# A gated feed-forward kernel: turned rows in two buffers, and turns, first product, second product and layer in pairs within a slot

## The chip, the cores and the metric

The kernel runs on one core of a Trainium2 chip. The metric is the device time of one execution in microseconds (us), here the median of the runs shown. The engines are named as in the profile: PE (TensorE), PEld (its weight loads), ACT (ScalarE), DVE (VectorE), POOL (GpSimd, which issues the indirect transfers) and SP (SyncE, which issues nearly all the others).

## What is computed

`x` is 16 batches of 512 rows of 512 numbers; `f` is 16 x 512 x 16 and `cond` is 16 x 512. In the reference, cut to what matters:

```
z   = (x @ f[b] / 512) @ f[b].T / 16
h   = gelu(x @ W.T + fc_bias + z + cond[b])
p   = softmax(h @ w_router + b_router)          # 16 experts
idx = top_k(p, 4)
y   = sum over e in idx of relu(h @ w1[e].T + b1[e]) @ w2[e]   # each expert is 128 wide
out = x + y + b2
```

An expert's rows are not known before the router has run, so they are collected by expert and computed in tiles.

## The kernel before

Products are made to full precision from two halves: a number is rounded to a high part by ACT (`ACT.Copy` into a float32r buffer), DVE subtracts it from the number for the low part, and PE makes three products (high by high, high by low, low by high).

The work runs in **slots** `s` = 0 to 100. The first 64 slots (`SLOTS`) each take one block of 128 rows, a quarter of a batch, through the layer: `lowrank_in` (L1044, once a batch), `layer` (L1060: 13 matmuls into one of two PSUM banks `lay`), `gelu` on ACT (L556), `turn_batch` (L1081, the block transposed on PE for the router), `take_batch` on ACT (L563), and by batch the router's softmax and choice on DVE and the counts on PE. Seven slots later POOL scatters the block's rows to the lists of their four experts in HBM (`place_rows`, L463, four indirect transfers), and the list of full tiles goes to a table there.

From slot 28 (`LAG`) on, slot `s` also works on **tile** `j = s - 28` of up to 512 rows of one expert, 72 in all (`NTILE`). The first 49 (`FULL`) have one expert; the other 23 are two halves of 256 rows with an expert each. The work of a tile is spread over three slots:
- `load_tile` (L310, SP) reads its number from the table, then loads its rows (1,056 KB) into one of two buffers `gr`, and its table row into `tabi`. It is issued in SP's slot `s` for tile `j + 2`.
- `turn_tile` (PE, L1146) transposes 128 rows of tile `j + 1` into one of two banks `trn`; `take_tile` (ACT L574, DVE L741) splits them into `gsb`, which is one buffer, so that ACT waits for `p_f1`, the first product of the tile before. `split_w1` (L580, L876) splits the expert's first weights, also after `p_f1`.
- `ffn1(j)` (L1162) is the first product: 12 matmuls (24 for two experts) into the bank `hid`. `hidden` (ACT, L601) adds bias and clips; `split_hidden` and DVE's `hidden` split it into `hh` and `hl`, one buffer each.
- `ffn2(j - 1, c)` (L1188) is the second product for a quarter `c`, into one of two banks `yps`; `result` copies it to `ys` (ACT for even `c`, DVE for odd), and POOL's `send` (L490) scatters it to `yt` in HBM.

What sets the order is one loop over `s` for each engine, written out by hand, with semaphores between. PE's order in a slot:

```
lowrank_in, layer(s), positions, router, turn_batch(s-1), counts, ffn1(j),
turn_tile(j+1,0), ffn2(j-1,0), turn_tile(j+1,1), ffn2(j-1,1), turn_tile(j+1,2), ffn2(j-1,2), turn_tile(j+1,3), ffn2(j-1,3)
```

`split_x(s + 4)` splits the block of `x` that is needed next but three; it stands near the start of ACT's and DVE's slot. `x` comes through two small buffers `stx`, and SP's loop begins each slot with `load_x(s + 6)` (L276):

```
def load_x(s):
    if s >= 4:
        sp.wait_ge(v_xl, s - 3 if s < 6 else s - 1)
    sp.dma_start(stx[:, x_buffer(s), :], xT[s]).then_inc(s_x[x_buffer(s)], 16)
```

So `load_x(s + 6)` waits until `split_x(s + 4)` is done on DVE (`v_xl`). Behind it, in order, SP has `load_u` and `load_v` (every fourth slot), some small copies, and `load_tile(j + 2)`.

After the last tile comes the **tail**: 32 sums of 256 rows, each of 2,048 KB of `yt`, plus `x` (512 KB) and `b2`, and out. `x` and `b2` are prepared ahead in the buffers `xin` (24 of the 32), 12 of them (`EARLY`) loaded from slot 80 on.

## Time and profile before

| | |
|---|---|
| Median of 3 runs | 1313.26 us (1309.89 to 1313.92) |
| Profiled execution: span, first to last instruction | 1288.1 us |
| Its own time as a run | not listed; the median is 25.2 us above the span |
| Busy: PE / DVE / ACT / POOL | 911.6 / 828.0 / 584.8 / 584.3 us |
| Granted TensorE clock, mean of the span | 0.869 |
| Moved by DMA | 354.82 MB, 275 GB/s over the span |

The span falls into four stretches: slots 0 to 27, the layer and the router alone (to about 197 us); slots 28 to 63, layer and tiles together (to about 699 us); slots from 64 on, tiles alone (to about 1067 us); and the tail. In a view by stretches, each engine has its busy time and number of instructions, and behind them stand the granted clock as a share of full speed, the busy share of the DMA engines, and GB/s. In a timeline, a row is start, duration, engine, line and operation, what is written from what is read, the count, and in brackets the engine's idle time before it with what ended that. "remote" there is a releaser that the profile doesn't show.

### The profile page before, as it was taken

To read this page: it belongs to the slowest core of one execution; us is meant where nothing else is said; L and a number is where in the kernel's file an instruction comes from. 1 tells how busy PE (TensorE), PEld (TensorE's weight loads), DVE (VectorE), ACT (ScalarE), POOL (GpSimd) and SP (SyncE) were. 2 spreads that over 40 slices of the span, in tenths; PEclk is the share of its full clock that TensorE was granted. 3 is DMA by queue.
4 is the path that set the end of the run, shared out by engine and by line. 5 is a ranking of instruction groups with operands and counts; after the bars stand their busy time and mean duration, and the time that the engine had idled before them with its cause. 6 is when DMAs were issued, how large, how long until landed. Compare 5 with 4: busy or idle time off the path is not lost.

```text
span 1288.1 us, 17916 instructions
## 1 busy us (share of the span) xinstructions
PE 911.6 (71%) x4924; PEld 702.2 (55%) x4924; DVE 828.0 (64%) x1964; ACT 584.8 (45%) x1061; POOL 584.3 (45%) x589
## 2 busy tenths in 40 slices
PE   8887789889899998888898774898898981000000
PEld 7664567677677766666676553677676761000000
DVE  4444355666556665556656563877687867987777
ACT  5434345565556555465546453765566560000000
POOL 1455664555565655555565655454455543000000
PEclk9988789989999999999999896999999996555555
DMA  5777577776787777777876765787888759999999
GB/s 173 266 241 272 190 245 278 263 258 228 252 272 264 252 263 256 246 259 242 269 261 235 254 237 220 239 261 236 288 271 259 232 166 357 414 429 429 426 430 385
DMA packets 103234, 354.82 MB, mean 275 GB/s; under 512 B 29961, under 2 KB 29961, under 8 KB 92384
## 3 DMA queue, kind: packets, MB, share of 16 engines
q1 hardware_dynamic: 59104, 217.21, 49.6%
q0 software_dynamic: 43936, 136.37, 27.0%
q8 instruction: 41, 0.67, 0.2%
q14 instruction: 57, 0.47, 0.1%
q10 hardware_dynamic: 96, 0.10, 0.0%
HBM read 200.47 MB, written 169.65 MB: 287 GB/s over the span
## 4 chain that ended last, share of the span: by engine, by line
PE 46%; another core or an unknown queue 13%; DMA 12%; DVE 11%; issue 8%; ACT 7%; ACTq 2%; DVEq 1%; POOL 0%; POOLq 0%; SPq 0%
PE yps L1201 10%; DMA w2l<-yt 10%; PE lay L1068 9%; PE trn L1158 8%; PE hid L1173 7%; PE hid L1178 4%; DVE gsb L744 3%; PE hid L1054 3%; PE trn L1088 2%; DVE stx L935 2%; ACT gsb L578 2%; DMA outT<-ys 2%; ACTq L589 1%; PE rps L1103 1%
## 5 line engine op out<-in xcount | busy, mean ns | idle before, releaser
L744 DVE TENSOR_TENSOR gsb<-trn,gsb 128x512 fp32r<-128x512 f32 x286 | 192.0, 687 | 258.3 <-ACT gsb L578 216.5
L498 POOL DMA_INDIRECT yt<-ys,ids x218 | 235.2, 1079 | 244.9 <-ACT ys L637 177.3
L472 POOL DMA_INDIRECT xg<-grow,ix x224 | 221.4, 988 | 139.6 <-DVE ix L818 74.2
L1158 PE MATMUL trn<-idf,gr 128*128 128x128 f32 x1144 | 185.6, 287 | 106.4 <-DVE gsb L744 101.1
L1158 PEld LDWEIGHTS trn<-idf,gr 128*128 128x128 f32 x1144 | 140.3, 146 | 170.1 <-DVE gsb L744 135.8
L1068 PE MATMUL lay<-w2l,xs 128*128 128x512 f32 x768 | 201.7, 414 | 0.0
L578 ACT ACTIVATE gsb<-trn 128x512 fp32r<-128x512 f32 x286 | 171.6, 600 | 30.1 <-PE trn L1158 16.5
L1068 PEld LDWEIGHTS lay<-w2l,xs 128*128 128x128 f32 x768 | 151.4, 201 | 33.1
L606 ACT ACTIVATE hv<-hid,b1c 128x512 f32<-128x512 f32 (+1 forms) x94 | 52.6, 584 | 222.6 <-PE hid L1178 106.8
L1201 PE MATMUL yps<-w2c,hh 128*128 128x512 f32 x368 | 140.6, 465 | 6.2 <-issue 4.5
L1173 PE MATMUL hid<-gsb,w1c 128*128 128x512 f32 (+1 forms) x576 | 133.2, 374 | 8.0 <-issue 7.8
L1173 PEld LDWEIGHTS hid<-gsb,w1c 128*128 128x128 f32 x576 | 95.9, 193 | 30.2 <-issue 9.6
L1201 PE MATMUL yps<-w2c,hl 128*128 128x512 f32 x184 | 77.8, 423 | 0.0
L919 DVE COPY ys<-yps 128x512 f32<-128x512 f32 x109 | 74.3, 682 | 3.8 <-PE yps L1201 2.3
L637 ACT ACTIVATE ys<-yps 128x512 f32<-128x512 f32 x109 | 65.7, 603 | 12.5 <-PE yps L1201 9.6
L1178 PE MATMUL hid<-gsb,w1c 128*128 128x512 f32 (+1 forms) x288 | 68.4, 360 | 0.0
L1201 PEld LDWEIGHTS yps<-w2c,hh 128*128 128x128 f32 x368 | 59.9, 204 | 10.2 <-issue 7.1
L561 ACT ACTIVATE grow<-lay 128x512 f32<-128x512 f32 x56 | 33.4, 597 | 68.5 <-PE lay L1073 44.5
L498 POOL DMA_INDIRECT yt<-stx,ids x40 | 45.2, 1130 | 42.2 <-ACT stx L637 25.1
L570 ACT ACTIVATE stx<-trn 128x512 f32<-128x512 f32 x64 | 38.1, 596 | 42.8 <-PE trn L1088 19.7
L614 ACT ACTIVATE hh<-hv 128x512 fp32r<-128x512 f32 x72 | 45.3, 629 | 25.9 <-PE yps L1201 13.9
L885 DVE TENSOR_TENSOR w1c<-w1f,w1c 128x512 fp32r<-128x512 f32 x72 | 49.4, 686 | 10.7 <-ACT w1c L591 9.5
(184 smaller groups left out, 1518.4 us busy)
## 6 DMA issues: line engine op xcount, KB each, us to landing
gr<-xg SPq DMA_DIRECT2D x49, 1056.0 KB
xs<-yt SPq DMA_DIRECT2D x16, 2048.0 KB, 19.5
w2l<-yt SPq DMA_DIRECT2D x15, 2048.0 KB, 19.7
gr<-xg SPq DMA_DIRECT2D x45, 528.0 KB
stx<-xT SPq DMA_DIRECT2D x64, 256.0 KB, 4.2
outT<-ys SPq DMA_DIRECT2D x31, 512.0 KB, 20.4
xg<-xrow SPq DMA_DIRECT2D x16, 528.0 KB
w2f<-xrow SPq DMA_DIRECT2D x16, 512.0 KB
```

What stands on the lines that cost most here:

```text
L472: pool.indirect_dma_start(out=xg, out_offset=bass.IndirectOffsetOnAxis(ap=ix[:, row_buffer(b), q, k:k + 1], axis=0), in_=grows[row_buffer( ...
L498: pool.indirect_dma_start(out=yt, out_offset=bass.IndirectOffsetOnAxis(ap=ids[:, j % 8, c:c + 1], axis=0), in_=yss[result_buffer(j)][:, c, ...
L578: act.activation(gsb[:, :, HI, c * P:(c + 1) * P], trn[n % 2][:, :].rearrange("p (k t) -> p k t", k=KC), ACT.Copy).then_inc(a_tn, 1)
L606: act.activation(hv[:, h * n:(h + 1) * n], hid[:, h * n:(h + 1) * n], ACT.Relu, bias=b1c[:, bass.DynSlice(e[h], 1)]).then_inc(a_hv, 1)
L637: act.activation(yss[result_buffer(j)][:, c, :], yps[c % 2][:, :], ACT.Copy).then_inc(a_y, 1)
L744: dve.tensor_tensor(gsb[:, :, LO, c * P:(c + 1) * P], trn[n % 2][:, :].rearrange("p (k t) -> p k t", k=KC), gsb[:, :, HI, c * P:(c + 1) * ...
L919: dve.tensor_copy(yss[result_buffer(j)][:, c, :], yps[c % 2][:, :]).then_inc(v_y, 1)
L1068: pe.matmul(lay[s % 2][:, :], xs[:, b % 2, k, h, cols], wls[:, k, a, :], start=(k == 0 and a == HI and h == HI), stop=False)
L1158: last = pe.transpose(trn[n % 2][:, k * P:(k + 1) * P], gr[:, j % 2, c, k * P:(k + 1) * P], idf[:, :])
L1173: pe.matmul(hid[:, cols], w1x[h][:, a, k * P:(k + 1) * P], gsb[:, k, HI, cols], start=(h == 0 and k == 0 and a == HI), stop=False)
L1178: last = pe.matmul(hid[:, cols], w1x[h][:, HI, k * P:(k + 1) * P], gsb[:, k, LO, cols], start=False, stop=(h == len(parts) - 1 and k == KC ...
L1201: last = pe.matmul(yps[c % 2][:, :], hx[:, c * P:(c + 1) * P], w[a], start=(i == 0), stop=(i == 2))
```

## The change

- `gsb` becomes three places of which two alternate (`home`): `gsb` itself for even tiles, and for odd tiles first one half of `xs`, later the old `gr` region. `take_tile` waits for the first product of the tile before the last one (`p_f1 >= j - 1`).
- `xs` loses that half: from batch 7 on `x` is split into the other half alone (`x_home`), in place, so that `split_x(s)` waits for `layer(s - 4)`.
- `hh`, `hl` and the second weights get a second buffer each (`hhs`, `hls`, `w2x`) in rows of `w2l` that come into use later; `split_w2(j)` moves from slot `j + 1` to slot `j`.
- From slot 66 on (`BANKS`) the second product uses four banks, `yps` and `lay`, one for each quarter (`result_bank`).
- From tile 45 on (`HOME` = 44) the rows of a tile are loaded into `grow`. The results have 3 buffers at most (5 before), `xin` 20 (24 before), and `EARLY` is 8 (12 before). The split of all second weights ahead (`presplit_w2`) is placed by a table.
- The loops of ACT, DVE and PE are written out anew for three ranges of slots. In slots 27 to 64 PE has: `turn_tile(j+1, 0)` and `(j+1, 1)`, `ffn1(j)`, `ffn2(j-1, 0)` and `(j-1, 1)`, `turn_tile(j+1, 2)` and `(j+1, 3)`, `lowrank_in`, `layer(s)`, `router`, `turn_batch(s-1)`, `ffn2(j-1, 2)` and `(j-1, 3)`. SP's and POOL's loops stay as they are.

The diff, cut to its core (functions that only have their buffer's name changed are left out, and DVE's loop, which mirrors ACT's):

```diff
-PRE = 46
+PRE = 48
 LATE = 36
-MORE = 39, 43, 55
-EARLY = 12
+HOME = 44
+BANKS = SLOTS + 2
+EARLY = 8
+PRESPLIT = {SLOTS + 2: (12, 13), SLOTS + 3: (14, 15), SLOTS + 8: (0, 1), SLOTS + 9: (2, 3, 8),
+            SLOTS + 10: (4, 5, 9), SLOTS + 11: (6, 10), SLOTS + 12: (7, 11)}
...
+def x_home(b):
+
+    return b % 2 if b < LAG // 4 else 1
...
+def home(j):
+
+    return 0 if j % 2 == 0 else 1 if j < HOME else 2
...
+def hidden_buffer(j):
+
+    return j % 2 if j < HOME else 0
...
+def second_buffer(j):
+
+    return j % 2 if j < HOME else 0
...
+def result_bank(j, c):
+
+    return c if j >= BANKS - LAG else c % 2
...
     for s in range(LAG + NTILE):
-        if 1 <= s <= SLOTS:
-            batch[s - 1] = n
-            taken.append(None)
-            n += 1
         if 0 <= s - LAG + 1 < NTILE:
             for c in range(chunks(s - LAG + 1)):
                 tile[s - LAG + 1, c] = n
                 taken.append(len(tile))
                 n += 1
+        if 1 <= s <= SLOTS:
+            batch[s - 1] = n
+            taken.append(None)
+            n += 1
...
+        ypss = yps + lay
+        gsbs = (gsb[:, :, :, :], xs[:, 0, :, :, :], gr[:, :, :, :].rearrange("p n q w -> p (n q w)")[:, 0:4 * KC * P * 2].bitcast(F32R).rearrange("p (k h t) -> p k h t", k=KC, h=2))
...
+        w2x = (w2c[:, :, :], w2l[:, 10:12, :])
+        hhs = (hh[:, :], w2l[:, 8, :])
+        hls = (hl[:, :], w2l[:, 9, :])
...
-        yss = (ys[:, 0, :, :], ys[:, 1, :, :], stx, grow[:, 0, :, 0:D], grow[:, 1, :, 0:D])
+        yss = (ys[:, 0, :, :], ys[:, 1, :, :], stx)
...
-               + [gr[:, n, 2 * m:2 * m + 2, 0:D] for n in range(2) for m in range(2)]
...
+        grs = [gr[:, n, :, :] if j <= HOME else grow[:, n, :, :] for j in range(NTILE) for n in [j % 2]]
...
             def split_x(s):
                 b, q = divmod(s, 4)
                 act.wait_ge(s_x[x_buffer(s)], x_in(s))
-                if b >= 2:
+                if b > LAG // 4:
+                    act.wait_ge(p_w, s - 3)
+                elif b >= 2:
                     act.wait_ge(p_w, 4 * (b - 1))
-                act.activation(xs[:, b % 2, :, HI, q * P:(q + 1) * P],
+                act.activation(xs[:, x_home(b), :, HI, q * P:(q + 1) * P],
...
             def take_tile(j, c):
                 n = TURN_TILE[j, c]
                 act.wait_ge(p_tn, n + 1)
-                if j > 0:
-                    act.wait_ge(p_f1, j)
-                act.activation(gsb[:, :, HI, c * P:(c + 1) * P],
+                if j == 1:
+                    act.wait_ge(p_w, LAG)
+                if j > 1:
+                    act.wait_ge(p_f1, j - 1)
+                if j == HOME + 1:
+                    act.wait_ge(v_id, HOME + 1)
+                act.activation(gsbs[home(j)][:, :, HI, c * P:(c + 1) * P],
...
             def split_hidden(j):
                 act.wait_ge(a_hv, per_half(j))
-                if j > 0:
-                    act.wait_ge(p_y, 4 * j)
+                if hidden_before(j) is not None:
+                    act.wait_ge(p_y, 4 * hidden_before(j) + 4)
...
+            for s in range(LAG - 1, SLOTS + 1):
                 b, q = divmod(s, 4)
                 j = s - LAG
+                for c in range(2):
+                    take_tile(j + 1, c)
+                if q == 2:
+                    likelihoods(b - 1)
+                if j >= 0:
+                    hidden(j, expert[j])
+                if j >= 1:
+                    result(j - 1, 0)
+                first_weights(j + 1)
+                for c in range(2, 4):
+                    take_tile(j + 1, c)
+                if q == 0 and b < NB:
                     split_z(b)
+                if j >= 0:
+                    split_hidden(j)
+                    split_w2(j, expert[j][0])
+                if q == 1 and b + 1 < NB:
+                    split_v(b + 1)
+                if s < SLOTS:
+                    gelu(s)
+                take_batch(s - 1)
                 if s + 4 < SLOTS:
                     split_x(s + 4)
                 if q == 3 and b + 1 < NB:
                     split_u(b + 1)
+                if j >= 1:
+                    result(j - 1, 2)
...
-                n = 4 * j + c
-                if n >= 2:
-                    pe.wait_ge(a_y if c % 2 == 0 else v_y, n // 2)
+                if result_bank(j, c) >= 2 and j == BANKS - LAG:
+                    pe.wait_ge(a_gel, SLOTS)
+                elif bank_before(j, c) is not None:
+                    i, d = bank_before(j, c)
+                    pe.wait_ge(a_y if d % 2 == 0 else v_y, 2 * i + d // 2 + 1)
...
+            for s in range(LAG - 1, SLOTS + 1):
                 b, q = divmod(s, 4)
                 j = s - LAG
+                for c in range(2):
+                    turn_tile(j + 1, c)
+                if j >= 0:
+                    ffn1(j)
+                if q == 0:
+                    positions(b - 2)
+                if j >= 1:
+                    for c in range(2):
+                        ffn2(j - 1, c)
+                for c in range(2, 4):
+                    turn_tile(j + 1, c)
                 if s < SLOTS:
                     if q == 0:
                         lowrank_in(b)
                     layer(s)
+                if s % 2 == 1:
                     router(s - 2)
+                turn_batch(s - 1)
+                if q == 3:
                     counts(b - 1)
+                if j >= 1:
+                    for c in range(2, 4):
+                        ffn2(j - 1, c)
+                if q == 1:
+                    turn_logits(b - 1)
+                if q == 2:
+                    ranks(b - 1)
+            for s in range(SLOTS + 1, LAG + NTILE + 1):
+                j = s - LAG
+                if j + 1 < NTILE:
+                    for c in range(2):
+                        turn_tile(j + 1, c)
...
+                if j < NTILE:
                     ffn1(j)
+                if j + 1 < NTILE:
+                    for c in range(2, chunks(j + 1)):
                         turn_tile(j + 1, c)
+                for c in range(chunks(j - 1)):
+                    ffn2(j - 1, c)
...
```

How the order moves, at three places. First PE in slot 47, a slot of both kinds of work (`hid` is the first product's bank, `trn` the turned rows, `yps` the second product). Before:

```order
L1068 MATMUL lay1<-w2l,xs 128x512 [waits a_gel]
L1073 MATMUL lay1<-w2l 128x512 [waits a_one,v_z,v_u]
L1103 MATMUL rps<-stx,wrz 32x256 [waits v_sv,a_tn]
L1088 MATMUL trn0<-idf,grow 128x128 [waits v_tn,a_gel]
L1173 MATMUL hid<-gsb,w1c 128x512 [waits a_hv,v_z,a_tn,v_w1]
L1158 MATMUL trn1<-idf,gr 128x128 [waits v_tn,s_gr_0]
L1201 MATMUL yps0<-w2c,hh 128x512 [waits a_y,v_w2,v_hl]
```

And with the change:

```order
L1294 MATMUL trn0<-idf,gr 128x128 [waits v_tn,s_gr_0]
L1294 MATMUL trn1<-idf,gr 128x128 [waits a_tn]
L1310 MATMUL hid<-xs,w1c 128x512 [waits a_hv,v_z,a_tn,v_w1]
L1341 MATMUL yps0<-w2c,hh 128x512 [waits a_y,v_w2,v_hl]
L1341 MATMUL yps1<-w2c,hh 128x512 [waits v_y]
L1294 MATMUL trn0<-idf,gr 128x128 [waits v_tn]
L1204 MATMUL lay1<-w2l,xs 128x512 [waits a_gel]
L1209 MATMUL lay1<-w2l 128x512 [waits a_one,v_z,v_u]
L1224 MATMUL trn0<-idf,grow 128x128 [waits v_tn,a_gel]
L1341 MATMUL yps0<-w2c,hh 128x512 [waits a_y]
```

The first turn, which waits for the tile's rows (`s_gr`), moved from behind layer and first product to the head of the slot.

Second, ACT (`grow<-lay` is `gelu`, `stx<-trn` `take_batch`, `xs<-stx` `split_x`, `gsb<-trn` `take_tile`). Before, from the `gelu` of slot 47 to that of slot 48:

```order
L561 ACTIVATE grow<-lay1 128x512 [waits p_w,s_sc_1_3]
L570 ACTIVATE stx<-trn0 128x4x128 [waits p_r,p_tn]
L606 ISA [waits v_hl,p_f1]
L606 ACTIVATE hv<-hid,b1c 128x512
L578 ACTIVATE gsb<-trn1 128x4x128 [waits p_f1,p_tn]
...
L614 ACTIVATE hh<-hv 128x512 [waits p_y,a_hv]
L554 ACTIVATE w2l<-hid 96x512 [waits p_w,p_z]
L534 ACTIVATE xs<-stx 128x4x128 [waits p_w,s_x_0]
L619 REGISTER_ALU [waits p_y]
L619 ACTIVATE w2c<-w2f 128x512
L561 ACTIVATE grow<-lay0 128x512 [waits p_w,s_sc_0_0]
```

And with the change, slot 47 from its head to `split_x`:

```order
L633 ACTIVATE gsb<-trn0 128x4x128 [waits p_f1,p_tn]
L633 ACTIVATE gsb<-trn1 128x4x128 [waits p_f1,p_tn]
L663 ISA [waits v_hl,p_f1]
L663 ACTIVATE hv<-hid,b1c 128x512
L690 ACTIVATE ys<-yps0 128x512 [waits s_y_0,p_y]
...
L671 ACTIVATE w2l<-hv 128x512 [waits p_y,a_hv]
L676 REGISTER_ALU [waits p_y]
L676 ACTIVATE w2l<-w2f 128x512
L612 ACTIVATE grow<-lay1 128x512 [waits p_w,s_sc_1_3]
L621 ACTIVATE stx<-trn0 128x4x128 [waits p_r,p_tn]
L585 ACTIVATE xs<-stx 128x4x128 [waits p_w,s_x_1]
```

`split_x` moved from ahead of the slot's `gelu` to behind it and behind `take_batch`.

Third, SP, whose order is the same in both kernels (line numbers of the changed one; `TENSOR_LOAD` is the read of the tile's number from the table in HBM):

```order
L331 DMA stx<-xT 128x512 [waits v_xl]
L374 TENSOR_LOAD table [waits s_tb]
L389 ISA [waits s_sc_1_0,s_sc_0_3,s_sc_1_1,s_sc_0_2,s_sc_1_2,s_sc_0_1,s_sc_1_3,s_sc_0_0,p_tn,s_sc_2_3,v_id,s_sc_2_2,v_w1,s_sc_2_1,s_sc_2_0]
L389 DMA gr<-xg 128x2112
L391 DMA tabi<-table 128x8
```

The tile's load stands behind the block's load, which waits for `split_x` (`v_xl`). Nothing moved here.

## Rows read from the trace of the kernel before

**Rows 1.** The view by stretches: layer and tiles, and the tail
```profile
197.00:699.00 502.00, 443.00 (x2340) 342.92 (x2343) 306.32 (x875) 286.30 (x509) 283.57 (x281) 0.96 0.74 254
...
1071.00:1288.00 217.00, 0.00 (x0) 0.00 (x0) 176.09 (x150) 0.00 (x0) 3.39 (x2) 0.51 0.98 412
```
**Rows 2.** The waits in the stretch 197 to 699 us: total, times, longest
```profile
ACT hv L606 <- remote: 82.7, 21, 5.2
...
PE trn L1158 <- DVE gsb L744: 57.8, 29, 2.9
```
**Rows 3.** The timeline of PE: end of the layer in slots 28 and 63
```profile
196.68 0.39 PE L1073 MATMUL lay<-w2l 98*128 98x512 f32 x1
...
698.53 0.39 PE L1073 MATMUL lay<-w2l 98*128 98x512 f32 x1
```
**Rows 4.** The timeline of PE in slot 59, which has no wait
```profile
640.46 3.00 PE L1068 MATMUL lay<-w2l,xs 128*128 128x512 f32 x12
643.30 0.39 PE L1073 MATMUL lay<-w2l 98*128 98x512 f32 x1
...
644.88 2.11 PE L1173 MATMUL hid<-gsb,w1c 128*128 128x512 f32 x8
...
647.74 0.60 PE L1158 MATMUL trn<-idf,gr 128*128 128x128 f32 x4
...
652.35 2.01 PE L1054 MATMUL hid<-xs,w2l 128*96 128x512 f32 x8
```
**Rows 5.** The timeline of ACT: `take_batch` behind the layer of slot 59
```profile
644.89 0.60 ACT L570 ACTIVATE stx<-trn 128x512 f32<-128x512 f32 x1 [0.23 <-issue]
```
**Rows 6.** The timeline: `split_x` on ACT and DVE, then SP
```profile
22.81 0.63 ACT L534 ACTIVATE xs<-stx 128x512 fp32r<-128x512 f32 x1
...
24.20 0.33 SPq L279 DMA_DIRECT2D stx<-xT  x1
```
**Rows 7.** The timeline of SP: a block's load and the tile's load behind it
```profile
262.42 0.33 SPq L279 DMA_DIRECT2D stx<-xT  x1
264.34 0.34 SPq L337 DMA_DIRECT2D gr<-xg  x1
...
568.62 0.33 SPq L279 DMA_DIRECT2D stx<-xT  x1
...
575.61 0.00 SPq L337 DMA_DIRECT2D gr<-xg  x1
```
**Rows 8.** The timeline: the load of tile 0, and who waited for it
```profile
182.37 0.00 SPq L337 DMA_DIRECT2D gr<-xg  x1
...
186.69 0.17 DVE L753 TENSOR_TENSOR above<-gr,tabi 128x12 f32<-128x12 int32 x1 [0.26 <-DMA tabi<-table]
```
**Rows 9.** The timeline of PE after two idle times, and a stretch
```profile
102.38 1.08 PE L1103 MATMUL rps<-stx,wrz 128*32 128x256 f32 x8 [5.29 <-ACT stx L570]
...
108.04 2.89 PE L1068 MATMUL lay<-w2l,xs 128*128 128x512 f32 x12
...
155.54 4.59 PE L1068 MATMUL lay<-w2l,xs 128*128 128x512 f32 x12
...
104.00:106.00 2.00, 2.00 (x8) 1.20 (x7) 1.15 (x7) 1.11 (x2) 1.39 (x3) 0.50 0.92 247
```
**Rows 10.** The timeline of PE in slots of two half tiles, tiles alone
```profile
880.55 1.18 PE L1173 MATMUL hid<-gsb,w1c 128*128 128x256 f32 x8
...
883.49 0.60 PE L1158 MATMUL trn<-idf,gr 128*128 128x128 f32 x4
...
890.05 1.19 PE L1173 MATMUL hid<-gsb,w1c 128*128 128x256 f32 x8
```
**Rows 11.** The chain of waits: first products of tiles 49 and 69
```profile
871.19 1.99 PE hid L1173 x16
...
1053.96 1.98 PE hid L1173 x16
```
**Rows 12.** The timeline of ACT: the longest wait between tiles
```profile
794.55 0.69 ACT L606 ACTIVATE hv<-hid,b1c 128x512 f32<-128x512 f32 x1 [18.23 <-remote]
```

348 lines of the change are left out of this document (209 added, 139 removed).

## The prediction

> **What bounds the kernel now.** I read the stretches first, then the waits, then slots of PE, and last SP. From slot 28 to 63 PE is busy for 443 of 502 us at a granted clock of 0.96, every other engine for less than 310, and the DMA engines for 0.74 of the time [rows 1]: PE leads, and what can be won there is its waits. Between the layer's ends of slots 28 and 63 lie 501.85 us for 35 slots, 14.34 us a slot [rows 3]. A slot without a wait takes 11.9 us: the layer starts at 640.46 and slot 60's first matmul at 652.35 [rows 4]. The rest is what the change aims at: PE waits 57.8 us for DVE's split of turned rows, 29 times, and ACT waits 82.7 us at `hidden` with a releaser that isn't shown [rows 2]; ACT can't take a turned block before the first product is done, and PE has two banks to turn into. In the slots with tiles alone the same ring makes 9.50 us from one first product to the next [rows 10]; from tile 49 to 69 the mean is (1053.96 - 871.19) / 20 = 9.14 us [rows 11]. The tail moves 412 GB/s at a DMA share of 0.98 [rows 1]: transfers bound it.
>
> **Term 1, slots of both kinds: a new ring through SP.** The two buffers take the wait away. But the order also moves two ends of one chain towards each other. `turn_tile(j+1, 0)`, which needs the tile's rows, goes to the head of PE's slot, ahead of first product and layer. `split_x(s+4)` goes behind `layer(s)`, `gelu` and `take_batch`; it has to wait for `layer(s)` now, since `x` is split in place. SP's order is unchanged: `load_x(s+6)` waits for `split_x(s+4)`, and `load_tile(j+2)` is queued behind it. The rows of tile `j + 2` are turned at the head of slot `s + 1`. So each slot is a closed ring: turn, first product, layer, gelu, `split_x`, SP, tile load, turn. Before, `split_x` came early and the turn late, so that a tile's rows had most of a slot to spare. Now nothing of the load is covered by anything but the rest of the second product. The ring, step by step:
> - From the turn to the layer's end on PE, at full clock. First product 647.74 - 644.88 = 2.86 us. Four pairs of turn and quarter of second product take 652.35 - 647.74 = 4.61 us; a turn of four transposes is 0.36 us, so a quarter product is 0.79, and four turns with two quarters are 3.02. Layer: 643.30 - 640.46 + 0.39 = 3.23 [rows 4]. `lowrank_in` has eight matmuls of the layer's width, about 1.85 us every fourth slot, 0.46 a slot. Sum 9.6 us. `turn_batch`, router and the other two quarters lie behind the layer, beside the chain, and cost nothing in it.
> - From the layer's end (643.69) to `take_batch` 1.2 us [rows 4, 5], in a slot with router; 1.0 taken. `split_x` starts 0.5 behind it, and from its start on ACT to SP's next issue pass 24.20 - 22.81 = 1.39 us, DVE's half included [rows 6]. Sum 2.9.
> - On SP, from the block's load to the tile's: the table is read and a dozen semaphores are waited for. 1.92 us at best and 6.99 in a slot with `load_u` and `load_v` [rows 7]. Part of the second is waiting for scatters and for PE, for which a longer slot leaves room; 3.4 taken, nearer the first.
> - The load itself: only tile 0's was waited for, 186.69 - 182.37 = 4.3 us [rows 8].
> - The clock. After 5.29 us of idle time the granted clock is 0.50, 1.2 GHz, and 5.66 us of matmuls run at that (102.38 to 108.04), which costs half of it, 2.8 us; after a shorter idle time a layer has 4.59 us for its twelve matmuls against 3.00, 1.6 lost [rows 4, 9]. In the ring PE has 11.9 us of work in a slot of 20 and more, so some 8 us idle; 2.3 taken.
>
> Together 9.6 + 2.9 + 3.4 + 4.3 + 2.3 = 22.5 us a slot against 14.3. SP's `load_x` ends with block 63, issued in slot 57; so the turns at the heads of slots 28 to 58 are in the ring, 30 periods: 30 x 8.2 = **+246 us**. At the start, slot 27's layer stands behind the turn of tile 0, which can't come before 186.69 [rows 8], and slot 28 waits for its first tile: four turns, the layer and the chain put slot 28's layer end near 215 against 197.07, **+17**. The five slots 59 to 63 are free: some 12.3 us each, **-10**.
>
> The Trainium skill (TensorE: Matmul & The Clock Gate, "HAM oscillation — how this bites in real kernels") describes just such a loop, a burst of matmuls shorter than the wait for its next load, and says that every burst then starts at the low clock. The rows after idle times agree; by it the clock's part would be paid in each slot, as taken. The skill (DMA: Bandwidth & Descriptors, "Anatomy of one DMA") gives 2.0 us and the bytes at 436 GB/s for a transfer; an estimate from that page is 4.5 us for the 1,056 KB, and the sum would be 6 us higher.
>
> **Term 2, tiles alone.** Here SP has no block to load, and `load_tile(j+2)` goes out as soon as tile `j` is turned, more than a slot ahead. The ring through `p_f1` is gone, so PE's work is left: 883.49 - 880.55 = 2.94 us for the first product [rows 10] and 4.6 for turns and second product [rows 4], 7.5; 7.6 taken. For the 22 steps between the 23 half tiles (9.14 - 7.6) x 22 = 34 us [rows 11]. The full tiles 36 to 48 gain less: the splits ahead of second weights fall into seven of their slots, and the wait of 18.23 us behind the last batch's scatters [rows 12] depends on POOL, whose loop is the same; some 24 at best. Of 58 I take **-50**, since other handoffs will show up. The four result banks and the second `hh`, `hl`, `w2c` belong here; apart from this they are free.
>
> **Term 3, the tail.** 20 buffers of `x` in place of 24: four loads of 512 KB more behind the last tile, 2.1 MB at 412 GB/s [rows 1], **+5**. The smaller `EARLY` only shifts loads within the slots with tiles.
>
> Against the profiled execution (span 1288) the sum is +17 + 246 - 10 - 50 + 5 = **+208 us**; put on the median, 1313 + 208 = 1521, and 1520 is forecast. About 0.3% is what a measurement of this kernel can tell from no change.
>
> **Rivals.**
> - *The tile's rows are in time* (the ring isn't closed, since SP gets ahead or the load is short). Then the slots of both kinds run at PE's pace, 12.1 us: 35 x 2.24 = -78, tiles alone -50, tail +5, start +4: 1194 us. For it speaks that PE's work is all that is left once `gsb` has two places. Against it, the load would have to land within 4.7 us of the layer's end, where the steps from the rows make 12.9. It decides as soon as the ring is below 14.3 us. Chance 0.07.
> - *The ring is closed but short*: PE keeps its clock, SP passes in 1.9 us, and parts overlap more than I see; 15 to 18.6 us a slot gives +20 to +129 on 30 slots, with the other terms -38, so 1296 to 1404. The bottom end of each step makes 9.6 + 2.9 + 1.9 + 4.3 = 18.7. Chance 0.08.
> - *The ring is longer*: SP needs its 6.99 us, the clock costs 2.8, and ACT's unexplained waits at `hidden` fall into it: 26 us and more, 30 x 11.7 - 38, 1626 us. Chance 0.05.
> - *The two buffers bring nothing with tiles alone*, because ACT's and DVE's work in order replaces the wait: 1570, inside the range.
>
> The forecast has the other 0.80. The range runs from the bottom of the steps, 1400, to 25 us a slot, 1313 + 30 x 10.7 - 38 = 1596, rounded up to 1605. Faster by over 0.3% is the first rival and a bit of the second, 0.08; within 0.3% 0.01; slower 0.91.
>
> **What would show it.** In the profile after, slots 28 to 58 should be 20 to 25 us apart by their layers, PE busy below 60% there at a clock well under 0.96, with one idle time of 7 us or more a slot that ends at the first turn; SP's tile load should stand 1.9 to 4 us behind the block's load, which starts at the end of `split_x` on DVE, and `take_ids` 4 to 5 us behind the tile load. `take_tile` should no longer follow the first product. Slots of half tiles should be 7.6 us apart. I am wrong if PE's turn at the slot's head doesn't wait, or waits for something else than the rows; right in kind but wrong in size if one step of the ring has another length.

## The result, and the profile after

| | before | after |
|---|---|---|
| Median (lowest to highest) | 1313.6 us (1309.9 to 1317.8), 4 runs | 1644.2 us (1630.9 to 1648.3), 4 runs |
| Profiled execution: span | 1288.1 us | 1646.3 us (as a run 1648.1) |
| Busy: PE / DVE / ACT / POOL | 911.6 / 828.0 / 584.8 / 584.3 us | 951.5 / 837.2 / 583.9 / 576.1 us |
| Granted clock, mean of the span | 0.869 | 0.785 |

The ratio is 1.265, with a 95% interval of 1.246 to 1.284. Forecast were 1520 us and a range up to 1605. The direction and the ring are as forecast; the size lies 124 us above the forecast and 39 above the range.

The chain that ended last, of the kernel after, by engine and by line. The second line now starts with a transfer that isn't named in the chain of before:

```profile
PE 39%; DMA 26%; issue 11%; DVE 8%; another core or an unknown queue 6%; SPq 5%; ACT 4%; POOL 1%; ACTq 1%; DVEq 0%; POOLq 0%
DMA tabi<-table 15%; PE hid L1310 9%; PE trn L1294 8%; PE lay L1204 8%; DMA w2l<-yt 8%; PE yps L1341 5%; PE hid L1315 3%; DVE xs L813 2%; PE hid L1190 1%; DVE stx L1026 1%; PE trn L1224 1%; ACT xs L585 1%; DMA outT<-ys 1%; PE lay L1341 1%
```

The view by stretches (columns as in [rows 1]): the ring's slots 28 to 58, 4 us at the head of slot 29, 4 us ahead of its layer's end, and the tail:

```profile
241.00:984.00 743.00, 427.92 (x2013) 343.18 (x2011) 273.17 (x755) 247.88 (x443) 250.66 (x243) 0.76 0.44 152
...
254.00:258.00 4.00, 3.62 (x13) 3.24 (x14) 1.89 (x5) 1.19 (x2) 0.00 (x0) 0.50 0.00 0
...
262.00:266.00 4.00, 4.00 (x26) 3.17 (x28) 3.83 (x7) 2.99 (x7) 2.81 (x2) 1.00 0.17 66
...
1427.00:1646.00 219.00, 0.00 (x0) 0.00 (x0) 176.07 (x150) 0.00 (x0) 1.54 (x1) 0.50 0.98 412
```

In the ring PE is busy for 428 of 743 us at a clock of 0.76, where [rows 1] had 443 of 502 at 0.96. Each slot begins at 0.50, 1.2 GHz, and ends at full clock. The waits in the ring's stretch, where [rows 2] had 57.8 us for `gsb` and 82.7 with an unshown releaser:

```profile
PE trn L1294 <- DMA tabi<-table: 315.1, 30, 13.0
DVE above L844 <- DMA tabi<-table: 256.7, 30, 11.5
```

30 waits, one a slot, all at the head of the slot and all for the tile's rows (the table's line is the last transfer behind them). The timeline of one turn of the ring, from the layer's end in slot 28 to that in slot 29, and the layer's ends of slots 58 and 63, which answer to [rows 3]:

```profile
240.50 0.40 PE L1209 MATMUL lay<-w2l 98*128 98x512 f32 x1
...
242.63 0.69 DVE L813 TENSOR_TENSOR xs<-stx,xs 128x512 fp32r<-128x512 f32 x1 [1.57 <-ACT xs L585]
243.35 0.33 SPq L331 DMA_DIRECT2D stx<-xT  x1
243.72 0.63 SPq L419 DMA_DIRECT2D xg<-xrow  x1
246.73 0.35 SPq L389 DMA_DIRECT2D gr<-xg  x1
...
254.35 0.17 DVE L844 TENSOR_TENSOR above<-gr,tabi 128x12 f32<-128x12 int32 x1 [11.03 <-DMA tabi<-table]
...
254.38 1.97 PE L1294 MATMUL trn<-idf,gr 128*128 128x128 f32 x8 [13.03 <-DMA tabi<-table]
...
265.62 0.39 PE L1209 MATMUL lay<-w2l 98*128 98x512 f32 x1
...
982.96 0.40 PE L1209 MATMUL lay<-w2l 98*128 98x512 f32 x1
...
1050.65 0.39 PE L1209 MATMUL lay<-w2l 98*128 98x512 f32 x1
```

From slot 28 to 58 pass (982.96 - 240.50) / 30 = 24.75 us a slot. The four steps of it, as means over the 30 slots: layer's end to `load_x` on SP 3.26, `load_x` to `load_tile` 2.37, issue to `take_ids` 7.32, `take_ids` to the next layer's end 11.80.

### The profile page after: what moved, and what is told of

Its sections match the earlier page's. It is cut to its first block, busy times and chain, and to the rows that moved or that the text cites. A ratio compares the mean times of both kernels' runs of the same rounds, so it can differ in the third digit from the quotient of the medians.

```text
span 1646.3 us, 17908 instructions
## 1 busy us (share of the span) xinstructions
PE 951.5 (58%) x4924; PEld 765.4 (46%) x4924; DVE 837.2 (51%) x1966; ACT 583.9 (35%) x1063; POOL 576.1 (35%) x589
## 4 chain that ended last, share of the span: by engine, by line
PE 39%; DMA 26%; issue 11%; DVE 8%; another core or an unknown queue 6%; SPq 5%; ACT 4%; POOL 1%; ACTq 1%; DVEq 0%; POOLq 0%
DMA tabi<-table 15%; PE hid L1310 9%; PE trn L1294 8%; PE lay L1204 8%; DMA w2l<-yt 8%; PE yps L1341 5%; PE hid L1315 3%; DVE xs L813 2%; PE hid L1190 1%; DVE stx L1026 1%; PE trn L1224 1%; ACT xs L585 1%; DMA outT<-ys 1%; PE lay L1341 1%
## 5 line engine op out<-in xcount | busy, mean ns | idle before, releaser
L1294 PE MATMUL trn<-idf,gr 128*128 128x128 f32 x720 | 127.8, 334 | 354.8 <-DMA tabi<-table 327.5
L633 ACT ACTIVATE gsb<-trn 128x512 fp32r<-128x512 f32 x144 | 81.0, 598 | 190.8 <-PE trn L1294 187.5
L633 ACT ACTIVATE xs<-trn 128x512 fp32r<-128x512 f32 x88 | 50.4, 597 | 211.5 <-PE trn L1294 160.5
L835 DVE TENSOR_TENSOR gsb<-trn,gsb 128x512 fp32r<-128x512 f32 x144 | 94.5, 686 | 55.4 <-ACT gsb L633 48.9
L1310 PE MATMUL hid<-gsb,w1c 128*128 128x512 f32 (+1 forms) x288 | 92.2, 478 | 1.7 <-DVE w2c L976 1.7
L835 DVE TENSOR_TENSOR xs<-trn,xs 128x512 fp32r<-128x512 f32 x88 | 58.6, 687 | 53.1 <-ACT xs L633 45.9
L1294 PE MATMUL trn<-idf,grow 128*128 128x128 f32 x424 | 60.6, 282 | 28.8 <-issue 10.8
L1341 PE MATMUL yps<-w2l 128*128 128x512 f32 x246 | 68.9, 418 | 0.0
L1294 PEld LDWEIGHTS trn<-idf,grow 128*128 128x128 f32 x424 | 47.3, 143 | 43.6 <-issue 26.6
L1310 PE MATMUL hid<-xs,w1c 128*128 128x512 f32 x176 | 67.0, 543 | 0.0
```

Source lines behind the costliest of these rows:

```text
L633: act.activation(gsbs[home(j)][:, :, HI, c * P:(c + 1) * P], trn[n % 2][:, :].rearrange("p (k t) -> p k t", k=KC), ACT.Copy).then_inc(a_tn, 1)
L835: dve.tensor_tensor(gsbs[home(j)][:, :, LO, c * P:(c + 1) * P], trn[n % 2][:, :].rearrange("p (k t) -> p k t", k=KC), gsbs[home(j)][:, :, ...
L1294: last = pe.transpose(trn[n % 2][:, k * P:(k + 1) * P], grs[j][:, c, k * P:(k + 1) * P], idf[:, :])
L1310: pe.matmul(hid[:, cols], w1x[h][:, a, k * P:(k + 1) * P], g[:, k, HI, cols], start=(h == 0 and k == 0 and a == HI), stop=False)
L1341: last = pe.matmul(ypss[result_bank(j, c)][:, :], hx[:, c * P:(c + 1) * P], w[a], start=(i == 0), stop=(i == 2))
```

## The experiments

The chips differ, and a column of the tables needs this first: on two chips the kernel before took 1123 us, on three others 1296 to 1312 us, near the 1314 us of the result above. What differs is told under "Held signals". Each ratio is to the kernel before on the same chip. "Slot" is the mean from layer's end 28 to 58, "tile" the mean from tile 49 to 70 by `split_hidden` (9.09 before, 9.12 after in the profiles shown).

### Is it the ring, and what are two buffers worth?

**e1_tile_first**, the changed kernel with one call moved in SP's loop:

```diff
                 j = s - LAG
+                if 0 <= j + 2 < NTILE:
+                    load_tile(j + 2)
                 if s + 6 < SLOTS:
                     load_x(s + 6)
...
-                if 0 <= j + 2 < NTILE:
-                    load_tile(j + 2)
```

> The changed kernel with one call moved: in SP's loop load_tile(j + 2) stands ahead of load_x(s + 6), load_u, load_v and the small copies. Theory of the ring (the tile's load is queued behind load_x, which waits for the slot's own layer): the ring opens, since the load now goes out as soon as tile j is turned and its first weights are split, a slot earlier. Slots 28 to 58 fall from 24.75 us to 12.5 to 14, 30 x -11 = -330, so 1290 to 1340 us, and PE's clock there is above 0.9. Rival A, the new order on PE, ACT and DVE is what costs (a lower clock, work in order): 1600 us or more. Rival B, transfers compete (the load itself takes long because of scatters and x): slots of 17 to 20 us, 1430 to 1500 us.

**e4_one_gsb**, on top of it:

```diff
 def home(j):
-    return 0 if j % 2 == 0 else 1 if j < HOME else 2
+    return 0
...
-                if j > 1:
-                    act.wait_ge(p_f1, j - 1)
+                if j > 0:
+                    act.wait_ge(p_f1, j)
```

> The kernel with the tile's load first, but one place for turned rows: home(j) = 0 for every tile and take_tile(j) waits for the first product of tile j - 1, as before the change; order, banks and second weights stay as changed. It prices the two buffers themselves. Theory: the turned rows can't be taken before the first product, PE waits 1 to 2 us a slot at turn_tile(j + 1, 2) or at ffn1, so 40 to 110 us above the kernel with the tile's load first. Rival, the new order already hides the split behind ffn2 and the layer, and the second buffer brings nothing in slots 28 to 63: within 10 us in that stretch.

| chip with before at 1123 us | us | ratio (95%) | slot | tile |
|---|---|---|---|---|
| e2_pads_behind (below; still the ring) | 1511.9 | 1.346 (1.341 to 1.351) | 23.82 | 8.69 |
| e1_tile_first | 1178.7 | 1.050 (1.046 to 1.054) | 12.79 | 8.53 |
| e4_one_gsb | 1218.6 | 1.085 (1.083 to 1.087) | 12.98 | 9.19 |

The view by stretches of e1_tile_first in slots 28 to 58, to be held against the 743 us above:

```profile
174.00:558.00 384.00, 363.90 (x2013) 291.59 (x2011) 267.31 (x755) 243.71 (x443) 248.34 (x242) 0.98 0.82 286
```

The same 2013 matmul instructions take 384 us, at a clock of 0.98. On the same chip e2_pads_behind, which leaves that call where it was, stays at 23.82 us a slot. So neither the order on PE, ACT and DVE nor the transfers by themselves hold the changed kernel at 24 us a slot: the place of one call on SP does. The low clock goes with the wait: it is a consequence of the ring and no cause of its own. The 1178.7 us are below what was expected only because the chip is another one; beside before it is still 5% slower.

Two buffers alone are worth 40 us (1218.6 - 1178.7). In slots 28 to 58 it is 0.2 us a slot, or 6 us, as the rival of the expectation had it; with tiles alone it is 0.66 us a tile, and 29 us lie there (359.9 against 331.1 us from slot 63 to PE's last matmul). In slots of both kinds the second buffer is hardly worth its place.

### The length of the load

**e2_pads_behind** and **e6_pads_late** take the copies `xg<-xrow` from ahead of the tile's load: behind it, or into SP's iterations 59 to 74.

The edit of e6_pads_late (e2_pads_behind moves `load_tile` alone, ahead of the unchanged copies):

```diff
-                if LAG <= s < LAG + 3 * NE and (s - LAG) % 3 == 0:
-                    e = (s - LAG) // 3
-                    sp.dma_start(xg[e * LREG:e * LREG + HALF, :],
...
                 if 0 <= j + 2 < NTILE:
                     load_tile(j + 2)
+                if SLOTS - 5 <= s < SLOTS - 5 + NE:
+                    e = s - SLOTS + 5
```

> The changed kernel with only the copies xg<-xrow (16 of 528 KB, 10 of them in the ring's slots) put behind load_tile in SP's loop. Ring theory: a load that follows such a copy takes some 3 us longer (9.3 against 6.4 us from issue to take_ids), every microsecond of it lies on the ring, so 10 x 3 = -30 us: 1605 to 1625. Rival, the loads are long for another reason (scatters in flight) and the copy only stands beside it: no change, 1644.

> The changed kernel with the 16 copies xg<-xrow moved out of the ring's slots altogether (one each in SP's iterations 59 to 74, behind load_tile). Against the changed kernel on the same chip: 10 slots of the ring lose some 3 us of load and 0.6 us of SP's issue: -30 to -36 us. Rival, the load behind such a copy is long for another reason: no change.

e6_pads_late took 1619.5 us (1597.4 to 1623.4) beside 1650.0 us (1639.3 to 1652.6) of e8_after_again, the unchanged kernel after on the same chip. In the ring the slot fell from 24.69 to 23.98, -21 us on 30 slots: 0.40 us a slot of it is the load (7.25 to 6.85 in the mean), 0.29 the step on SP. The loads of the ten slots fell from 8.3 to 7.3 us and not to the 6.7 of the others, so the expected 3 us a load were 1; the 9.3 and 6.4 us of the expectation were single loads, and the means are 8.4 and 6.8. Ahead of the ring 19 us are gone as well (slot 27: 202.1 against 221.4), which is no proof of anything, see below, and slots 59 to 63, where the copies went, take 6 us more. For e2_pads_behind nothing stands beside it on its chip but before; its slot of 23.82 us agrees.

The rival of the expectation, scatters in flight, is not ruled out by this; the trace speaks for it too. In the kernel after, of the loads without a copy ahead, the 6 in whose time POOL issued at most one transfer took 5.8 us in the mean, and the 14 with four or five took 7.2. Of the ten with a copy ahead, the 3 with at most one took 6.7, the 7 with four or five 9.1. Two single loads show the parts. Tile 1 of the kernel after has a block's load ahead of it and no scatter beside it:

```profile
223.16 0.33 SPq L331 DMA_DIRECT2D stx<-xT  x1
224.62 0.34 SPq L389 DMA_DIRECT2D gr<-xg  x1
...
229.74 0.17 DVE L844 TENSOR_TENSOR above<-gr,tabi 128x12 f32<-128x12 int32 x1 [4.73 <-DMA tabi<-table]
```

Tile 1 of e13_after_gaps (below) has nothing of SP's for 11.1 us ahead and nothing behind but its table line, but four scatters beside it:

```profile
176.28 0.33 SPq L332 DMA_DIRECT2D stx<-xT  x1
187.38 0.34 SPq L390 DMA_DIRECT2D gr<-xg  x1
...
193.49 0.17 DVE L855 TENSOR_TENSOR above<-gr,tabi 128x12 f32<-128x12 int32 x1 [15.30 <-DMA tabi<-table]
```

They took 5.1 and 6.1 us, where tile 0 of the kernel before, with neither, took 4.3 [rows 8]. So a block ahead and scatters beside seem each to lengthen the load. No run moved the scatters alone, and the chips of the two differ, so the shares stay open.

### Tiles alone

**e3_tables4** (on e1_tile_first) and **e10_after_tab4** (on the kernel after) give the table's line four places:

```diff
-        tabi = sb("tabi", [P, 2, 2, 4], I32)
+        tabi = sb("tabi", [P, 4, 2, 4], I32)
...
-                    sp.wait_ge(v_w1, per_half(j - 2))
+                    if j >= 4:
+                        sp.wait_ge(v_w1, per_half(j - 4))
```

> The kernel with the tile's load first, and four places for the tile's table line (tabi) in place of two, so that load_tile(j) no longer waits for the first weights of tile j - 2, only for its turns and ids. Theory: with tiles alone a second ring goes turn, first weights, load, turn over two slots, (8.7 + 9.5) / 2 = 9.1 us; now the load goes out some 3 us earlier, a half tile takes 7.6 to 8 us and the whole is 25 to 50 us below the kernel with the tile's load first. Rival, ACT's and DVE's own work or the results' way out sets 9.1 us: no change against it.

> The changed kernel with four places for the table line alone, SP's order as changed. Ring theory: in slots 28 to 58 nothing changes, since load_tile is held by load_x ahead of it and not by v_w1: 24.7 us a slot. With tiles alone the load goes out some 3 us earlier: -20 to -25 us where before takes 1123 us, 0 to -10 where it takes 1311. Rival: v_w1 is the last wait in the ring too, then 30 slots lose 1 us or more each, -30 and more in that stretch.

e3_tables4: 1162.4 us, ratio 1.036 (1.034 to 1.039), a tile 7.99 us in place of 8.53. With tiles alone there was a second ring, as expected, but the whole is 16 us below e1_tile_first, where 25 to 50 were expected. The timeline of the kernel after shows it, DVE's split of first weights, SP's loads, and PE at the head of the next slot but one:

```profile
1249.33 0.69 DVE L976 TENSOR_TENSOR w2c<-w1f,w2c 128x512 fp32r<-128x512 f32 x1
1250.26 0.88 SPq L389 DMA_DIRECT2D grow<-xg  x2
...
1251.19 0.42 SPq L391 DMA_DIRECT2D tabi<-table  x1
1251.67 0.42 SPq L398 DMA_DIRECT2D w2f<-xrow  x1
...
1260.37 1.94 PE L1294 MATMUL trn<-idf,grow 128*128 128x128 f32 x8 [2.80 <-DMA tabi<-table]
```

The load of a tile waits until the weights of the tile before the last one are split, because the table's line has two places; then it takes 10.1 us until PE can turn. e10_after_tab4, on a chip with before at 1296 us: 1622.5 us, ratio 1.255 (1.247 to 1.263), a tile 8.97, a slot 24.85. So in the ring `v_w1` isn't the last wait, as expected, and on that kind of chip the fix gives a tile only 0.1 us.

### Held signals

**e7_before_again** is the kernel before unchanged, **e8_after_again** the kernel after.

> The kernel before, unchanged, profiled on the chip of these runs. In the first group of runs it took 1123 us, against 1313 us in the runs and the profile shown. Theory A: the waits whose releaser the profile doesn't show (82.7 us of them in slots 28 to 63, 13% of the chain that ended last) belong to the chip or to the conditions of the first profile, not to the program; then a profile at 1123 us has none or few of them, the other rows (first product 2.9 us, layer 3.2 us, slot without wait 11.9 us) stay, and slots 28 to 63 are some 12.5 us apart. Rival B: the chip is faster throughout (the granted clock, the transfers): then the durations of single rows differ too. If it lands at 1313 us again, the waits are there again.

> The changed kernel, unchanged, on the same chip as the runs beside it, so that they can be compared. Where the kernel before takes 1123 us, the ring should still give 23 to 24 us a slot in slots 28 to 58 (its steps are SP's, the transfer's and PE's), the other slots should lose their unexplained waits, and the whole should be 1510 to 1550 us, a ratio of 1.35 to 1.38 in place of 1.265. Rival: the chip's conditions stretched the ring too, and it falls below 22 us a slot, 1450 us or less. On a chip where before takes 1313 us: 1644 us again.

This chip was one with before at 1311 us: e7_before_again 1292.1 us, e8_after_again 1650.0 us, ratio 1.254 (1.246 to 1.263). Two things follow. The same kernel came out at a ratio of 0.982 (0.974 to 0.990) to itself; on such a chip differences of 2% between two kernels mean nothing, and 0.3% was too fine a bound. And the waits with an unshown releaser are back: added up over the view of waits they are 225 us here and 220 in e8_after_again, 229 in the profile shown of before, 213 after; on the two chips with before at 1123 us the view has none in any of seven kernels, four of them without memsets (below). In the four profiles with such waits named here, each is one of ACT or DVE for a semaphore that PE raises. Rival B of the expectation, a chip that is faster throughout, is out: the medians of single rows are the same on both kinds of chip (in e8_after_again and e2_pads_behind a matmul of the first product 0.393 us, `gelu` 0.597, a scatter to `xg` 0.960), and so is the tail, 225.0 and 224.8 us.

What such a wait looks like, in slot 13, where the order is that of before, by PE's last layer matmul, POOL's scatters and ACT's `gelu`. First e8_after_again:

```profile
84.28 0.39 PE L1209 MATMUL lay<-w2l 98*128 98x512 f32 x1
...
85.41 0.97 POOL L521 DMA_INDIRECT xg<-grow,ix  x1 [0.30 <-issue]
...
94.67 0.96 POOL L521 DMA_INDIRECT xg<-grow,ix  x1 [0.30 <-issue]
97.33 0.60 ACT L612 ACTIVATE grow<-lay 128x512 f32<-128x512 f32 x1 [10.67 <-remote]
```

Then e2_pads_behind, on the other kind of chip, in the midst of the same run of scatters:

```profile
73.44 0.39 PE L1209 MATMUL lay<-w2l 98*128 98x512 f32 x1
...
73.92 0.60 ACT L612 ACTIVATE grow<-lay 128x512 f32<-128x512 f32 x1 [1.69 <-PE lay L1209]
...
74.66 0.96 POOL L521 DMA_INDIRECT xg<-grow,ix  x1 [0.30 <-issue]
```

From the matmul's end to `gelu` pass 12.7 us against 0.1; the first `gelu` starts 1.7 us after POOL's eighth scatter in a row is over. **e11_scatters_spaced** puts two small memsets behind each scatter of the first six batches of the kernel before, **e12_before_gaps** behind every scatter, **e15_before_gap1** one memset in place of two, **e13_after_gaps** and **e18_after_gap1** the same in the kernel after:

```diff
+            def gap(n):
+                for _ in range(n):
+                    gaps[0] += 1
+                    pool.memset(idle[:, :], 0.0).then_inc(g_s, 1)
+                    pool.wait_ge(g_s, gaps[0])
...
                         in_=grows[row_buffer(b)][:, q, :], in_offset=None).then_inc(s_sc[row_buffer(b)][q], 16)
+                    gap(2)
...
                     oob_is_err=False).then_inc(s_y[result_buffer(j)], 16)
+                gap(2)
```

> The kernel before with two chained small memsets on POOL (some 0.7 us) behind each scatter of the first six batches, nothing else. It asks what the waits with an unshown releaser are: on one chip ACT's gelu of slots 13, 17, 21 and 25 starts 10 to 13 us after the layer's last matmul, while POOL issues 8 or more scatters one right behind the other, and the signal comes 1.2 to 1.7 us after the last of them; on the other chip the same run of scatters delays nothing. Theory A: PE's signals are held back while POOL issues scatters back to back (on chips where before takes 1311 us); with gaps they get through, the waits of 10 us in slots 13 to 26 go, and slot 27 ends 10 to 30 us earlier. Rival B: not the run but the number of scatters counts, or the wait is for the scatters' own completion: the waits stay or grow, since POOL is slower, and slot 27 ends at the same time or later. On a chip where before takes 1123 us: no such waits in either, slot 27 later by what POOL loses.

> The kernel before with two chained small memsets on POOL behind every scatter (xg and yt), some 0.3 to 0.6 us more from one scatter to the next. Theory A, signals are held back while POOL issues scatters one right behind the other: on a chip where before takes 1290 to 1311 us the waits with an unshown releaser fall from 225 us to below 80, slots 28 to 63 from 14.4 to 12.5 to 13.2 us each, slot 27 ends 20 to 25 us earlier, and the whole is 60 to 100 us shorter (1200 to 1240). Rival B, as with gaps in the first six batches alone, the time comes back elsewhere (POOL's own pace, 8 scatters of 1.6 us a slot, takes the place of the wait): within 20 us of before. Where before takes 1123 us: 0 to 20 us slower.

> The changed kernel with the same gaps behind every scatter. Theory A: the ring stays (it has no such wait among its steps): 23.8 to 24.5 us a slot from 28 to 58, as where before takes 1123 us; slot 28's layer ends 25 to 50 us earlier than in the changed kernel (241 to 244 us); with tiles alone 8.8 us a tile in place of 9.1. Together 1560 to 1600 us. Rival B: the late start and the 9.1 us belong to the change itself: 1620 us or more.

> The kernel before with one memset behind every scatter in place of two. Theory A: a short gap is enough if any other instruction of POOL lets the signals through: then as good as with two memsets or better by some us; if the length of the gap counts, the waits shrink by half only, and it lies between before and the kernel with two.

> The changed kernel with one memset behind every scatter. The same edit in the kernel before gave a ratio of 0.95 to before. Theory: the ring is unchanged, 23.8 to 24.5 us a slot from 28 to 58, and the start and the tiles alone get what they can without held signals: slot 28 near 200, 8.5 to 8.8 us a tile; 1570 to 1605 us, a ratio of 1.20 to 1.23 to before, 1.27 to 1.29 to the kernel before with the same edit. Rival: the ring itself contains held signals, and falls below 23 us a slot: 1550 or less.

| | before on this chip | us | ratio (95%) | slot 27 / 28 ends | slot | tile | unshown waits |
|---|---|---|---|---|---|---|---|
| e7_before_again | 1311 | 1292.1 | 0.982 (0.974 to 0.990) | 182.8 / 198.2 | 14.46 | 9.05 | 225 us |
| e11_scatters_spaced | 1296 | 1291.7 | 0.997 (0.994 to 1.001) | 158.4 / 174.9 | 14.94 | 9.00 | 115 us |
| e12_before_gaps | 1312 | 1336.6 | 1.022 (1.016 to 1.027) | 158.2 / 174.6 | 15.93 | 8.88 | none |
| e15_before_gap1 | 1312 | 1247.1 | 0.953 (0.946 to 0.959) | 169.4 / 186.6 | 13.51 | 8.80 | 79 us |
| e8_after_again | 1311 | 1650.0 | 1.254 (1.246 to 1.263) | 221.4 / 244.0 | 24.69 | 9.00 | 220 us |
| e13_after_gaps | 1312 | 1605.8 | 1.225 (1.217 to 1.233) | 173.2 / 205.4 | 24.19 | 8.44 | none |
| e18_after_gap1 | 1123 | 1560.1 | 1.391 (1.387 to 1.395) | 157.9 / 186.8 | 24.09 | 8.39 | none |

Breaking the runs of scatters takes the waits away, all of them with two memsets (e18_after_gap1 says nothing of this: its chip holds no signals anyway). The sums are from different chips, and on the one with before at 1312 us no kernel without memsets was profiled; that it is of the holding kind is seen by the 79 us of e15_before_gap1. So the runs of scatters hold the signals. Whether the length of the gap or the other kind of instruction in it lets them through, and why some chips hold nothing at all, stays open. In e11_scatters_spaced the 24 us won by slot 27 are but 5 in slot 29 (203.2 against 208.1): PE waits 16.3 us for tile 1's rows, whose load stands behind POOL's now slower scatters. In e12_before_gaps POOL bounds every slot (in slots 30 to 58 its transfers start 1.93 us apart in the mean, 15.4 us for eight), so rival B of its expectation is right in kind, though the run is 24 us above before and not within 20. The chain that ended last, by engine:

```profile
POOL 46%; issue 26%; DMA 17%; DVE 5%; PE 3%; SPq 1%; POOLq 1%; ACT 1%; ACTq 0%; DVEq 0%
```

One memset is the better dose, 4.7% below before on the one chip it ran on; but here too POOL is near its limit, as its timeline shows (start to start 1.4 us behind `xg`, 1.9 behind `yt`, some 13 us for the eight of a slot):

```profile
303.14 0.98 POOL L508 DMA_INDIRECT yt<-ys,ids  x1 [0.79 <-POOL idle L471]
304.10 0.13 POOL L471 MEMSET idle<- 128x4 f32 x1
305.01 0.98 POOL L508 DMA_INDIRECT yt<-ys,ids  x1 [0.78 <-POOL idle L471]
...
309.40 0.98 POOL L481 DMA_INDIRECT xg<-grow,ix  x1 [0.28 <-issue]
310.38 0.12 POOL L471 MEMSET idle<- 128x4 f32 x1
310.77 1.02 POOL L481 DMA_INDIRECT xg<-grow,ix  x1 [0.28 <-POOL idle L471]
```

The ring is 24.1 to 24.2 us a slot in e13_after_gaps and e18_after_gap1, and held signals are no part of the 24.7 without memsets either: in slots 28 to 58 the kernel after has no wait with an unshown releaser, e8_after_again 3.4 us of them in all. What e13_after_gaps has less is load (6.98 for 7.32 us) and the handoff from the layer to SP (3.06 for 3.26). e18_after_gap1 was expected at 1570 to 1605 us, on the other kind of chip; 1560.1 us, 8.39 us a tile and slot 28 at 187 are all a little below that.

### Can a version beat both?

**e5_tile_earlier** is e3_tables4 with `load_tile(j + 3)` in place of `load_tile(j + 2)` at the head of SP's loop; **e14_earlier_gaps** adds two memsets behind every scatter (and has three places for the table's line). **e9_hybrid** keeps the loops, `home(j) = 0` and `x_home(b) = b % 2` of before up to slot 64, and has the loops of after from slot 65 on, with four table places. **e16_before_half_gaps** is the kernel before and **e17_hybrid_half_gaps** the hybrid (with three table places), both with one memset behind every second scatter:

```diff
+                    if k % 2 == 1:
+                        gap(1)
...
+                if c % 2 == 1:
+                    gap(1)
```

> Four places for the table line and load_tile(j + 3) ahead of load_x(s + 6), an iteration of SP earlier than in the kernel with the tile's load first. That kernel lost 21 us slots at slots 36 and 48 and 14 us ones at others, where the tile's load stood behind load_u, load_v and a copy of the iteration before. Theory: these go, slots 28 to 63 take 12.0 to 12.4 us each against 12.7, and the whole is 10 to 25 us below the kernel with four table places (1162 us where before takes 1123). Rival A: the loads then meet the scatters or wait on SP for scatters of the last batch and hold up load_x behind them, so that split_x comes late: no gain or a loss. Rival B: PE's own work sets the pace and nothing changes.

> Up to slot 64 the order of the kernel before (one place for turned rows, x split into both halves of xs, SP as it was); from slot 65 on the changed kernel's order, with two places for turned rows and four result banks, and four places for the table line. Theory: slots 28 to 63 are bounded by PE's work and by the waits that no buffer removes, so the new order has nothing to win there and only makes the ring; what it wins is with tiles alone, where 9.14 us became 8.0 us with four table places on the chip of the first runs. So this one is 20 to 35 us faster than before on a chip where before takes 1123 us (ratio 0.97 to 0.98), less (0 to 20 us) where before takes 1311, since a half tile took 8.9 us there even with four table places. Rival: the half tiles' pace needs all of the changed order, or the tail (4 loads of x more) takes it back: ratio 1.00 or above.

> The changed kernel with load_tile(j + 3) ahead of load_x(s + 6), three places for the table line, and the gaps behind every scatter. Without gaps it took 1335 us beside 1311 of before, with 15.0 us a slot from 28 to 63 and 9.0 a tile alone, and 298 us of waits with an unshown releaser. Theory A: 12.3 to 13.3 us a slot, 8.0 to 8.5 a tile, 1180 to 1230 us, faster than before by 5 to 9%. Rival B: POOL's pace (8 scatters and gaps a slot, 13.5 us and more) bounds it: 1260 to 1320.

> The kernel before with one memset behind every second scatter. With one behind each, POOL's 8 scatters of a slot take 13.6 us (1.4 to 1.9 us each) and slots 28 to 63 went 13.6 us apart, so POOL sets the pace there. With half the memsets: 11 to 12 us of POOL's time a slot. If two scatters in a row hold a signal for 2.5 us at most, slots fall to 12.5 to 13.2 us and the whole to 1205 to 1235 us (0.92 to 0.94). Rival: two in a row are enough to hold the signals until the third or longer, then it lies between 1247 and 1312.

> The order of the kernel before up to slot 64, the changed one from slot 65 on, three places for the table line, one memset behind every second scatter. Theory: with the held signals gone the second place for turned rows pays where tiles are alone, 8.1 to 8.5 us a tile against 8.8 to 9.1 in the kernel before with gaps: 10 to 25 us below the kernel before with the same gaps, less 5 us of tail. Rival: as on the chip where it took 1322 us beside 1296, something at the switch or in the tail takes it back: no gain.

| | before on this chip | us | ratio (95%) | slot | tile |
|---|---|---|---|---|---|
| e5_tile_earlier | 1311 | 1334.8 | 1.016 (1.009 to 1.022) | 14.96 | 8.93 |
| e9_hybrid | 1296 | 1322.1 (1295.0 to 1332.5) | none given | 14.40 | 8.92 |
| e14_earlier_gaps | 1312 | 1350.2 | 1.030 (1.024 to 1.037) | 14.90 | 8.53 |
| e16_before_half_gaps | 1123 | 1152.1 | 1.026 (1.023 to 1.028) | 12.59 | 8.45 |
| e17_hybrid_half_gaps | 1123 | 1162.5 | 1.036 (1.033 to 1.039) | 12.66 | 7.97 |

None of the five is faster than before on the chip it ran on, and none ran on both kinds of chip. The expected gains of e5_tile_earlier and e14_earlier_gaps didn't come; the first has 298 us of held signals, and in the second POOL sets the pace (1.91 us from transfer to transfer, 15.3 us for eight, in slots 30 to 58). e9_hybrid decides nothing: its six runs spread over 38 us, and the lowest is level with before. On a chip that holds no signals a memset behind every second scatter costs 2.6%; whether it would pay on the other kind, as e16_before_half_gaps was meant to show, no run tells. e17_hybrid_half_gaps does win 10 us between tiles 49 and 70, and gives them back around it: from tile 35 to 48 it is 8 us slower, and from PE's last matmul to the end it takes 229 us against 219. On a chip with before at 1312 us, e15_before_gap1 is the one version that beats both.

## Why the prediction was wrong in size

By the terms of its sum, from the two profiled executions (1646.3 - 1288.1 = 358 us):

| term | forecast | measured |
|---|---|---|
| start, slot 28's layer end | +17 | 240.9 - 197.1 = +44 |
| 30 periods of the ring | +246 | 30 x (24.75 - 14.37) = +311 |
| slots 59 to 63 | -10 | 67.7 - 70.8 = -3 |
| tiles alone, to PE's last matmul | -50 | 370.3 - 371.0 = -1 |
| tail | +5 | 225.0 - 218.2 = +7 |
| sum | +208 | +358 |

The 24.75 us of the ring lie within the 25 that the range allowed for. The range moved with the ring alone and took the start and the tiles as exact, and these two are 76 us off. Slots 59 to 63 take 59.0 us on a chip without held signals (e2_pads_behind), near the 12.3 us each of the forecast.

**The mechanism was right.** The two ends of the chain were moved towards each other and closed a ring over SP; e1_tile_first opens it with one call, and the ring's slots fall to 12.79 us (from 23.8 on that chip). PE's share (58%), SP's 2.4 us between the two loads and the wait at the first turn are as the prediction's last part had them.

**"The load itself: 4.3 us" is the step that failed in the ring.** It measures 7.32 us in the mean of 30. The other steps sum to 17.4 us, where 18.2 were forecast: handoff 3.26 for 2.9, SP 2.37 for 3.4 (near the lower of the two rows it was taken from), PE with its clock 11.80 for 11.9. The 4.3 us came from tile 0 [rows 8], the one load that was waited for. In the trace of before SP had issued nothing for 5.7 us ahead of it, and POOL issued no scatter in its first 3.7 us. In the ring `load_x` is always issued some 2.4 us ahead, every third slot also the copy of 528 KB, and in 21 of 30 loads POOL issues four or five scatters in the load's time; without the copy 6.7 to 6.8 us pass, with it 8.3 to 8.4. That the load is what was mis-sized is shown; how its 3 us divide between what is ahead of it and the scatters beside it is not. The step is +3.0 us a slot, or 91 us on 30, of which the other steps give 23 back. The Trainium skill (DMA: Bandwidth & Descriptors, "Anatomy of one DMA — SWDGE (gpsimd) path") has a fit for a transfer that GpSimd issues, which by estimate is 4.5 us for this size; here SP issues it. Tile 0's 4.3 us are near that, but the shortest load in the ring took 5.0, the trace disagrees there, and it is the measured 7.3 that decides.

**The clock was right.** The forecast paid 2.3 us a slot. PE's step with it came within 0.1 us; the rows show 0.50 at the slot's head after 13 us of idle time and 1.00 by the layer, and from the turn on the clock stands at 0.50 for 4.7 us of a slot in the mean, which at half speed costs 2.3. The Trainium skill (TensorE: Matmul & The Clock Gate, "HAM oscillation — how this bites in real kernels") says of bursts of matmuls between such waits that each starts at the low clock; the trace agrees, and so does e1_tile_first, at 0.98 without the wait.

**The start, +17 for +44.** Up to slot 26 both kernels have the same order, and yet slot 26 ends at 206.8 against 176.9 us. In the timeline of the kernel after, slot 25's layer is done at 186.27; ACT's `gelu` waits till 195.37, late in a run of POOL's of 16 scatters and a table (175.5 to 197.0), so a signal can also get through before the run is over:

```profile
185.88 0.39 PE L1209 MATMUL lay<-w2l 98*128 98x512 f32 x1
...
195.37 0.60 ACT L612 ACTIVATE grow<-lay 128x512 f32<-128x512 f32 x1 [8.61 <-remote]
...
196.04 0.96 POOL L521 DMA_INDIRECT xg<-grow,ix  x1 [0.30 <-issue]
...
199.63 0.60 ACT L621 ACTIVATE stx<-trn 128x512 f32<-128x512 f32 x1 [3.67 <-remote]
```

These 30 of the 44 us are held signals. On the chips that hold none, slot 26 ends at 137.0 to 139.1 us in kernels of either order, and with both kernels' runs of scatters broken at 154.6 (e12_before_gaps) and 155.2 us (e13_after_gaps). How far they hit a run varies (slot 26 at 190.2 in e6_pads_late, at 208.0 in e8_after_again, the same code up to there). But all six profiles of changed kernels without memsets on such chips end it at 190 to 208 us and both of before at 177 to 179, so it may not be chance alone; the cause stays open. From slot 26 to 28 the kernel after takes 34 us and before 20, +14; on the two chips without held signals it is 40 (e2_pads_behind) against 20 (e16_before_half_gaps). So the waits for tiles 0 and 1, which the +17 stood for, measure +14 to +20, and that term was right in its mechanism. (e13_after_gaps has 50 us there, since its memsets push the scatters and with them tile 1's load, which goes out 11.1 us behind the block's load, 1.5 in the kernel after.)

**Tiles alone, -50 for -1.** "The ring through `p_f1` is gone, so PE's work is left" took the wait for the whole. First, another ring was there, through `v_w1`: I wrote that the load goes out "as soon as tile `j` is turned", and the code had it wait for the weights of tile `j` as well, with a load that takes 10 us and not 4. On the chip without held signals this is worth 0.5 us a tile, on the other kind only 0.1. Second, a part of the 9.14 us was held signals: the kernel before takes 8.45 us a tile with half the runs broken on a chip without them (e16_before_half_gaps), and two memsets take the kernel after from 9.00 to 8.44 on the kind that has them. What two buffers and three table places give from 8.45 is 0.5 us a tile (e17_hybrid_half_gaps, 7.97), and 7.6 was never reached.

**The rivals.** "Two buffers bring nothing with tiles alone" was true of the size, though not for its reason. "The ring is longer" (1626 us, chance 0.05) was nearest; but of its three reasons none held: SP needed 2.37 us and not 6.99, the clock cost 2.3 and not 2.8, and held signals are absent from the ring. It was the load. Its chance was too low because I had bounds for each step but the load, for which one row stood at both ends. And against the first rival the prediction set 12.9 us from the layer's end to the landing; without the clock, which is paid on PE, its steps make 10.6, still far above the 4.7 that were there.

**The gain that was never there.** I read a slot without a wait as 11.9 us and the rest, 2.4 us, as "what the change aims at". Of [rows 2] the larger wait had no releaser, and I let both go with the buffers. With broken runs on a chip that holds nothing, the kernel before is at 12.59 us a slot (and there POOL's eight transfers alone take 12.1), and with one memset on a chip that does at 13.51, where 79 us of such waits are left: most of that rest was held signals, as far as different chips can be compared, and no buffer of turned rows touches them.

## What to carry to other kernels

When an edit moves a consumer to the head of a slot and a producer to its end, follow every in-order queue from the one to the other; a load that had a slot to spare may now be behind a wait for that very slot, and the cure is the order of two calls on that queue. Take a load's length from rows where as much is in flight ahead of it and beside it as there will be after the change; the one load that was ever waited for may be the one that had least beside it. Give every term of the sum its own range, also those that seem settled. And a large wait whose releaser the profile doesn't show is no gain to be booked until something makes it go.

## What the runs showed of the hardware

- **Held signals.** On four of six occasions (the result above, and the chips with before at 1311, 1296 and 1312 us) signals of PE reach ACT and DVE late, by 12.7 us in the row shown and some 18 in the wait of [rows 12], while POOL issues scatters 0.30 us after one another; with one small chained memset behind each scatter the sum of these waits was 79 us, beside 225 without on another such chip, and the time 4.7% shorter; with two it was none. On two chips with the same program there is no such wait and before takes 1123 us, 14% less.
- **Identical kernels, not identical times.** On a chip with held signals one kernel differed from itself by 1.8% with an interval that excludes 1. There a small difference has to be read from stretches of the trace, not from the total.
- **A load's time is that of its company.** The same 1,056 KB took 4.3 us with nothing of SP's for 5.7 us ahead and no scatter issued in its first 3.7 us, 5.1 behind a block of 256 KB issued 1.5 us earlier, and 6.1 with four scatters beside it. In the ring the mean was 5.8 us with at most one scatter and 7.2 with four or five, 6.7 and 9.1 with a copy of 528 KB ahead as well.
